# The first attention of a two-layer decoder, reordered into pairs and quads of heads

## What is computed

```python
scores = jnp.einsum('bhtd,bhsd->bhts', q, k) * ATTNSCALE          # q and k after rope
key_self = jnp.clip(jnp.sum(k * k, axis=-1), 1e-06, None)
w = jax.nn.softplus(scores / jnp.sqrt(key_self)[:, :, None, :])
w = jnp.where(causal, w, 0.0)
w = w * jax.nn.sigmoid(SCALE * w)
w = jnp.where(w < sinks, 0.0, w)
total = jnp.sum(w, axis=-1, keepdims=True) + sinks + 1e-06
out = jnp.einsum('bhts,bhsd->bhtd', w / total, v) + (sinks / total) * v_null
y = mean over the branches of (context @ W_O + W_O_bias)
```

## Time and profile before

| | us |
|---|---|
| time before, median of 3 runs (lowest to highest) | 3647.07 (3644.27 to 3649.19) |
| the profiled execution, its own time | 3643.7 |
| its span from the first to the last instruction | 3642.0 |
| first start of L434 and of L651 | 64.0, 67.0 |
| last start of L651 | 1119.5 |
| layer norm behind the first attention starts | 1188 |

### The profile page before, as it was taken

How to read it: one execution, slowest core, us unless ns; L and a number is a source line. 1 busy time by engine, 2 the same in 40 slices (tenths; PEclk the granted TensorE clock), 3 DMA queues, 4 the chain that set the end, 5 groups by cost and what they waited for, 6 DMA issues and landing times. The chain is left out here.

```text
span 3642.0 us, 51017 instructions
## 1 busy us (share of the span) xinstructions
PE 3184.4 (87%) x16640; PEld 2118.5 (58%) x16640; DVE 2152.4 (59%) x4638; ACT 1572.6 (43%) x2705; POOL 895.5 (25%) x1150
## 2 busy tenths in 40 slices
PE   5899999999987455898997999999999899986998
PEld 3334334334432343666665268888888677755887
DVE  3998898898885444655654134444444544445544
ACT  3665665665662212444443133333333455543211
POOL 2333334333331000444443000000000355550000
PEclk9999999999997666999998589999999899997999
DMA  2000000000000102010012000000000200001000
GB/s 87 3 4 1 3 3 0 3 3 0 3 1 1 38 23 61 20 37 23 21 37 56 0 4 3 3 3 3 3 3 5 75 6 6 3 29 59 6 6 26
DMA packets 88113, 61.03 MB, mean 17 GB/s; under 512 B 54800, under 2 KB 76560, under 8 KB 87504
## 3 DMA queue, kind: packets, MB, share of 16 engines
q1 hardware_dynamic: 88016, 59.93, 5.5%
HBM read 41.03 MB, written 8.39 MB: 14 GB/s over the span
## 5 line engine op out<-in xcount | busy, mean ns | idle before, releaser
L1727 POOL TENSOR_SCALAR x_weights<-x_weights,x_sums 128x256 f32<-128x256 f32 x256 | 231.7, 923 | 1061.6 <-DVE x_sums L1764 1061.6
L632 DVE SCALAR_TENSOR_TENSOR a_w<-a_w,a_sinks 128x256 f32<-128x256 f32 (+1 forms) x1024 | 466.3, 515 | 3.2
L434 ACT ACTIVATE a_e<-psum 128x1536 f32<-128x1536 f32 x128 | 185.6, 1450 | 385.6 <-PE psum L401 385.3
L318 PE MATMUL psum<-a_w,a_v 128*17 128x512 f32 x512 | 273.7, 617 | 85.4 <-DVE a_sumT L623 67.9
L1029 POOL TENSOR_SCALAR f_weights<-f_weights,f_sums 128x256 f32<-128x256 f32 x256 | 232.1, 924 | 294.8 <-DVE f_sums L1259 294.8
L476 POOL TENSOR_SCALAR_AFFINE_SELECT a_w<-a_w 128x512 f32<-128x512 f32 x256 | 180.1, 725 | 383.9 <-DVE a_w L651 383.8
L1456 ACT ACTIVATE a_weights<-psum,a_negmax 128x1024 f32<-128x1024 f32 x128 | 142.6, 1114 | 293.1 <-DVE a_negmax L1496 293.1
L399 PE MATMUL psum<-a_qT,a_kT_head 128*128 128x512 f32 x512 | 251.7, 614 | 7.7 <-DVE a_w L651 5.0
L1430 PE MATMUL psum<-a_v,a_turned_w 128*128 128x128 f32 x2048 | 248.3, 275 | 0.0
L651 DVE SCALAR_TENSOR_TENSOR a_w<-a_e,psum 128x1536 f32<-128x1536 f32 x128 | 223.9, 1749 | 24.9 <-ACT a_e L436 22.2
L1430 PEld LDWEIGHTS psum<-a_v,a_turned_w 128*128 128x128 f32 x2048 | 238.1, 192 | 0.0
(11 more groups left out here) (300 smaller groups left out, 6913.6 us busy)
## 6 DMA issues: line engine op xcount, KB each, us to landing
a_xnT<-all_xnT_all SPq DMA_DIRECT2D x16, 256.0 KB, 2.3
x_ctxT<-in_x_ctxT SPq DMA_DIRECT2D x16, 256.0 KB, 2.7
f_xnT<-all_xnT_all SPq DMA_DIRECT2D x16, 256.0 KB, 2.3
f_pv_rows<-f_pv SPq DMA_DIRECT2D x8, 512.0 KB, 2.8
f_pv_groups<-f_pv_rows SPq DMA_DIRECT2D x8, 512.0 KB
f_w<-in_f_w SPq DMA_DIRECT2D x2, 2048.0 KB, 10.4
all_x_all<-in_x SPq DMA_DIRECT2D x1, 2048.0 KB, 8.5
a_wq<-in_a_wq SPq DMA_DIRECT2D x2, 1024.0 KB, 10.4
```

Source lines behind the costliest of these rows:

```text
L318: pe.matmul(psO[0:DH + 1, :], v1[:, 0, u, :], w[:, u % RING, half * 512:(half + 1) * 512], start=True, stop=False)
L434: act.activation(e[:, j % 2, :], psS[j % 2], ACT.Exp).then_inc(exp_done, 1)
L632: ins = dve.scalar_tensor_tensor(part, part, sinks[:, r * NH + u:r * NH + u + 1], part, ALU.is_ge, ALU.mult)
L1727: ins = pool.tensor_scalar(w, w, sums[:, k, h, t:t + 1], None, ALU.mult)
```

## The change

Heads are worked in pairs (eight steps a batch, three slots a step) and summed in quads.

- **Scores.** The pair of step s is head 4*(s//2) + s%2 and that head plus two. Each lies in 32 rows of its own; `kT_half` holds k twice, with the even and with the odd heads' rows zero, so that a product uses 32 rows instead of 128. A slot is two PSUM banks, 1024 columns: slots 0 and 1 hold two branches each of both heads (first 128 keys, 256 queries), slot 2 all four branches of both (last 128 keys, last 128 queries). There are three such slots in place of two groups of three banks.
- **Causal part.** A further product, of the identity and a matrix with -1e30 above the diagonal, both float32r, is added onto the scores of each bank. The selections of GpSimd go.
- **ScalarE** takes exponential and logarithm by slot, 1024 columns, 24 times a batch; silus come in bursts of four heads at the first slot of every even step, once the last merge of the step before is there.
- **VectorE** merges by slot (two instructions of 512 columns in slots 0 and 1, one of 1024 in slot 2), runs the 16 thresholds of a quad (one of 384 columns for each head and branch) in one piece at the first slot of an even step, and copies sums of 128 x 512 after the first and second slot of odd steps.
- **Sums.** For four heads, each half is four products of 32 columns on 32 partitions of their own in bank 6, then four more for the last keys.
- The order written out by hand becomes `BESIDE_SLOT`. In it TensorE scores slot x of step s+1 after the side items of (s, x), and needs the merge of (s, x) for it; in odd steps a half of the sums follows that score.
- GpSimd masks k four times a batch, not sixteen.

```diff
-NU = NH
-RING = 8
-K1 = BR * T
-UNIT = BR * T + BR * P
+PAIRS_OF_HEADS, QUADS, SLOTS = NH // 2, NH // 4, 3
+PAIR_RING = 4
...
-SOFTPLUS_LAG, THRESHOLD_LAG, SUM_LAG = 1, 6, 8
-SILU_EVERY, SILU_FROM, SILU_TO = 4, 5, 2
...
+BESIDE_SLOT = {(0, 0): [("q", 0, HERE)], (0, 1): [("q", 1, HERE)], (0, 2): [("q", 2, HERE)],
+               (1, 0): [("q", 3, HERE)], (1, 1): [("regroup", 4, OLD), ("regroup", 5, OLD)], (1, 2): [("k", 0, AHEAD)],
+               (2, 0): [("k", 1, AHEAD)], (2, 1): [("v", 0, HERE)],
+               (3, 0): [("regroup", 6, OLD), ("regroup", 7, OLD)], (3, 1): [("norm", 0, AHEAD)], (3, 2): [("q", 0, AHEAD)],
+               (4, 0): [("q", 1, AHEAD)], (4, 1): [("q", 2, AHEAD)], (4, 2): [("q", 3, AHEAD)],
+               (5, 0): [("turn", 0, OLD)], (5, 1): [("turn", 1, OLD)], (5, 2): [("turn", 2, OLD)],
+               (6, 0): [("turn", 3, OLD)], (6, 1): [("out", 0, OLD)], (6, 2): [("regroup", 0, HERE), ("regroup", 1, HERE)],
+               (7, 0): [("regroup", 2, HERE), ("regroup", 3, HERE)]}
...
+def quad_at(b, at, new, old):
+    if at >= 0:
+        return (at, b * QUADS + at) if new else None
+    return (QUADS + at, b * QUADS + at) if old else None
...
-        psS = [psum[:, 3 * i:3 * i + 3, :].rearrange("p k n -> p (k n)") for i in range(2)]
+        psS = [psum[:, 2 * x:2 * x + 2, :].rearrange("p k n -> p (k n)") for x in range(SLOTS)]
...
+            def score_slot(bb, step, x):
+                n, g = bb * PAIRS_OF_HEADS + step, step // 4
+                if x == 0 and step % 4 == 0:
+                    pe.wait_ge(kheads_ready, bb * 2 + g + 1)
+                    pe.wait_ge(rotated, bb * ROTATED + 6 + 4 * g)
+                if not isinstance(n, int) or n > 0:
+                    pe.wait_ge(capped, (n - 1) * SLOTS + x + 1)
+                heads = [4 * (step // 2) + step % 2 + 2 * h for h in range(2)]
+                rows = [slice(32 * (u % 8 // 2), 32 * (u % 8 // 2) + 32) for u in heads]
+                if x < 2:
+                    for h in range(2):
+                        pe.matmul(psum[:, 2 * x + h, :], kT_half[rows[h], step % 2, g, 0:P], qT[rows[h], g, 2 * x:2 * x + 2, :],
+                                  start=True, stop=False)
+                    for h in range(2):
+                        ins = pe.matmul(psum[:, 2 * x + h, :].rearrange("p (r t) -> p r t", r=2)[:, :, 0:P], ident_r[:],
+                                        future[:].unsqueeze(1).to_broadcast([P, 2, P]), start=False, stop=True)
+                else:
+                    for h in range(2):
+                        pe.matmul(psum[:, 4 + h, :], kT_half[rows[h], step % 2, g, P:T], qT[rows[h], g, :, P:T],
+                                  start=True, stop=False)
+                    for h in range(2):
+                        ins = pe.matmul(psum[:, 4 + h, :].rearrange("p (r t) -> p r t", r=BR), ident_r[:],
+                                        future[:].unsqueeze(1).to_broadcast([P, BR, P]), start=False, stop=True)
+                ins.then_inc(scored, 1)
...
+            def sum_half(b, quad, half):
+                k, n = quad
+                if k == 0 and half == 0:
                     pe.wait_ge(v_taken, b + 1)
                 pe.wait_ge(weights_done, n + 1)
                 wait(pe, sums_taken, 2 * n + half)
-                pe.matmul(psO[0:DH + 1, :], v1[:, 0, u, :], w[:, u % RING, half * 512:(half + 1) * 512],
-                          start=True, stop=False)
-                lo = K1 + half * 256
-                pe.matmul(psO[0:DH + 1, :].rearrange("p (r t) -> p r t", r=2)[:, :, P:T], v1[:, 1, u, :],
-                          w[:, u % RING, lo:lo + 256].rearrange("p (r t) -> p r t", r=2), start=False, stop=True)\
-                  .then_inc(summed, 1)
+                for tile in range(TT):
+                    for h4 in range(4):
+                        branches = w[:, (2 * k + h4 % 2) % PAIR_RING, h4 // 2, 2 * half:2 * half + 2, :]
+                        out = psO[VCOLS * h4:VCOLS * h4 + VCOLS, :].rearrange("p (r t) -> p r t", r=2)
+                        cols, to = (slice(0, T), out) if tile == 0 else (slice(T, COLS), out[:, :, P:T])
+                        ins = pe.matmul(to, v1[:, tile, 4 * k + h4, :], branches[:, :, cols], start=(tile == 0),
+                                        stop=(tile == TT - 1))
+                ins.then_inc(summed, 1)
...
+                        spare_free = [(out_taken, bb + 1)]
+                for step in range(PAIRS_OF_HEADS):
+                    quad = quad_at(b, (step - 3) // 2, new, old) if step % 2 else None
+                    for x in range(SLOTS):
+                        for kind, i, when in BESIDE_SLOT.get((step, x), []):
+                            if exists[when]:
+                                pass_through_spare(kind, i, when)
+                        if step < PAIRS_OF_HEADS - 1 and new:
+                            score_slot(b, step + 1, x)
+                        elif step == PAIRS_OF_HEADS - 1 and ahead:
+                            score_slot(b + 1, 0, x)
+                        if quad and x < 2:
+                            sum_half(b, quad, x)
...
+                for step in range(PAIRS_OF_HEADS):
+                    for x in range(SLOTS):
+                        n = (b * PAIRS_OF_HEADS + step) * SLOTS + x
+                        if new:
+                            act.wait_ge(scored, n + 1)
+                            act.activation(e[:, x, :], psS[x], ACT.Exp).then_inc(exp_done, 1)
+                            act.wait_ge(exp_done, n + 1)
+                            act.activation(e[:, x, :], e[:, x, :], ACT.Ln, bias=1.0).then_inc(ln_done, 1)
+                        for kind, i, when in BESIDE_SLOT.get((step, x), []):
+                            if exists[when]:
+                                take_turned(kind, i, when)
+                        if ahead and (step, x) == (3, 2):
+                            act.wait_ge(norm_taken, b + 2)
+                            act.activation(ksq[:], ksq[:], ACT.Ln).then_inc(ln_k, 1)
+                            act.wait_ge(ln_k, b + 2)
+                            act.activation(ksq[:], ksq[:], ACT.Exp, scale=-0.5, bias=ln_quarter[:, 0:1]).then_inc(knorm_ready, 1)
+                        quad = quad_at(b, step // 2 - 1, new, old) if (step % 2, x) == (0, 0) else None
+                        if quad:
+                            k, n = quad
+                            act.wait_ge(capped, (n * 2 + 2) * SLOTS)
+                            for pair in range(2):
+                                for h in range(2):
+                                    wu = w[:, (2 * k + pair) % PAIR_RING, h].rearrange("p r t -> p (r t)")
+                                    act.activation(wu, wu, ACT.Silu, scale=SILU_SCALE).then_inc(silu_done, 1)
                             act.preload_act_table_set("natural_log_exp_and_others")
...
-            def head_rows(g, first, last):
-                for u in range(8 * g + first, 8 * g + last):
-                    ins = pool.tensor_scalar(kT_head[:, u, :], kT[:, g, :], head_mask[:, u % 8:u % 8 + 1], 1.0,
+            def head_rows(g):
+                for odd in range(2):
+                    ins = pool.tensor_scalar(kT_half[:, odd, g, :], kT[:, g, :], parity[:, odd:odd + 1], 1.0,
                                              ALU.mult, ALU.mult)
-                    if u % 8 == 7:
-                        ins.then_inc(kheads_ready, 1)
+                ins.then_inc(kheads_ready, 1)
...
+            def take_sums(quad, half):
+                k, n = quad
+                dve.wait_ge(summed, 2 * n + half + 1)
+                if half == 0:
+                    wait(dve, regrouped, (n - 1) * 2)
+                dve.tensor_copy(sumT[:, k % 2, half * 512:(half + 1) * 512], psO).then_inc(sums_taken, 1)
+            def threshold(quad):
+                k, n = quad
+                for pair in range(2):
+                    for h in range(2):
+                        dve.wait_ge(silu_done, n * 4 + 2 * pair + h + 1)
+                        for r in range(BR):
+                            part = w[:, (2 * k + pair) % PAIR_RING, h, r, :]
+                            col = r * NH + 4 * k + pair + 2 * h
+                            ins = dve.scalar_tensor_tensor(part, part, sinks[:, col:col + 1], part, ALU.is_ge, ALU.mult)
+                ins.then_inc(weights_done, 1)
...
+                for step in range(PAIRS_OF_HEADS):
+                    summed_quad = quad_at(b, (step - 3) // 2, new, old) if step % 2 else None
+                    silu_quad = quad_at(b, step // 2 - 1, new, old) if step % 2 == 0 else None
+                    for x in range(SLOTS):
+                        n = (b * PAIRS_OF_HEADS + step) * SLOTS + x
+                        if new:
+                            if x == 0 and step % 2 == 0:
+                                wait(dve, summed, (b * QUADS + step // 2 - 1) * 2)
+                            dve.wait_ge(ln_done, n + 1)
```

(38 more changed lines are left out.)

167 lines of the change are left out of this document (32 added, 135 removed).

## The result

| | before | after |
|---|---|---|
| time, median (lowest to highest) | 3645.8 us (3644.3 to 3649.2) | 3693.3 us (3682.0 to 3699.2) |
| ratio, 95% interval | | 1.0127 (1.0103 to 1.0151) |
| span of the profiled execution | 3642.0 | 3697.3 |
| main part, first exponential to end of the last merge | 1057.2 | 1130.7 |
| tail behind it, to the end of the last addition onto x | 66.7 | 39.2 |

What follows compares the result with a forecast made beforehand. TensorE and VectorE fill the first attention before; afterwards no engine is full and the strict order decides. Eight batches of 132.4 us less 21 give 1038 against 1057, the tail 43 against 66.7: 43 off, 3604 us, range 3500 to 3690.

Steps and rivals of the forecast that it cites:

- the clock's charge: TensorE work behind the hole in three of four quads runs at the lower clock: 2 us each, 6 a batch.
- Its bound, 139 a batch: Upper end for a batch: 13 us of TensorE's chain work at the lower clock throughout, less the 2 charged.
- Rival C: First attention: the clock stays down through the odd step, 5 us more a quad, +20 a batch, 3764 us; chance 0.11.
- The walk's total: First attention: following the strict order through a batch's four quads at the priced engine times gives 126.4 us a batch.
- VectorE's sum 86: VectorE's work in a batch of the first attention falls from 124 to 86 us.
- ScalarE's 86: ScalarE's batch work: exponentials and logarithms 49 us, silus with table loads 33, with small ones some 86.
- the hole of 7.4 us: TensorE idles 7.4 us waiting for the merge behind the 16 thresholds, in three of four quads.
- the score slot 1.5: TensorE takes 1.5 us for each of the first two score slots, 1.7 for the third.
- the copies' idle time of 3.1 us twice a quad: VectorE idles 3.1 us at each copy of sums while TensorE scores, then sums; twice a quad.
- TensorE's 87 us: TensorE's batch work in the first attention: scores 38 us, sums 12, other matmuls 37, together 87.
- Rival B: Column tiles of the sums don't run four abreast: +10 a batch, 3684 us, or +30, 3840; chance 0.11.
- Rival A: Orders interlock better, so the longest engine sets a batch: 86 becomes some 97 us, time 3321; chance 0.10.

Runs made afterwards that it cites:

- e6_warm: Changed kernel plus idle TensorE products in every larger gap: 8 or 4 a hole, one in each odd-step gap and between two regroupings; 3590.2 us.
- e8_rows128: Changed kernel with score products taking all 128 rows in place of 32, running one after another; 3701.7 us.
- e9_again32: Changed kernel with each pair of 32-row score products issued twice, the second overwriting the first; 3912.7 us.
- e1_fill7: Changed kernel with seven idle fp32 products in TensorE's hole before the score of slot 1 in steps 0, 2 and 4; 3687.6 us.
- e10_oddonly: Changed kernel with idle products only in the odd steps' gaps and between two regroupings of step 1, holes left empty; 3708.4 us.

## Why the prediction was wrong

**The step that failed** is the clock's charge: "I charge 2 us for each such quad ... That is 6 a batch". By the account it is 21.9 a batch, half of 43.8; by batches alone, 144.5 less the 124.5 at clock 1.00 in e6_warm, 20.0. Two things were wrong in the step. It took only the work right behind a hole, "about 4 us", while the clock stayed low 5.5 to 14.8 us into the work. And it took holes alone, while the clock also falls behind gaps of 1.4 to 2 us in the odd steps. Its bound, 139 a batch, was passed as well.

Rival C came nearest, with +20 a batch on top of the 6, but not quite as it was put: its sign was that the passes stay at twice their length until the next burst, and in most quads the clock comes back and falls again; only the stretch at 677.26 is of C's kind. The argument against it ("keeps TensorE almost without a gap for 14 us, and today's stage, with gaps of its own, stands at 0.99") did not look at how long the falls last. Today's stage has them too, 3.4 us each; in the steady batch of the changed kernel they last 6.8 us and more. Today's scores use 128 rows, the new ones 32, and e8_rows128 against e9_again32 shows that this matters. C's price was somewhat too high and its chance, 0.11, too low.

**What held.** The walk's total: 126.4 a batch forecast, 124.5 in the batch of e6_warm at clock 1.00 with the change's own order, 122.6 by the chain's account of the changed kernel. That it came so near is partly luck. From one silu burst to the next that batch takes 32.4, 30.5, 33.8 and 27.8 us in steps 0 and 1, 2 and 3, 4 and 5, 6 and 7, where the walk had 32.8, 30.3, 30.4 and 32.9: 3.4 too little in one quad and 5.1 too much in another. (The changed kernel itself, with its clock, has 40.1, 37.1, 37.2 and 28.9.) VectorE's sum 86 (85.7), in which the thresholds are 36 us and not 34, the merges 30 and not 29 (the prediction's own prices add up to 30), and the takes that stay, by difference, 14 and not 18. ScalarE's 86 (84.9), the hole of 7.4 us (7.9), the score slot 1.5 (1.48), the copies' idle time of 3.1 us twice a quad (3.2). TensorE's 87 us at full speed cannot be read from a busy time of 106.3 at 0.77.

Rival B falls: half a quad's sums cost 1.43 us, where one head's took 1.40, so four column tiles run side by side without loss. By the Trainium skill (TensorE: Matmul & The Clock Gate, Part 3), which has 2.38 times for three tiles, I had estimated 0.35 us more a half; the measurement decides against that here. Rival A falls too: no batch of this order came under 122 even without cold time.

**The sum again**, in spans. Predicted 3599 (3642.0 less 43), measured 3697.3, so 98.3 off. Clock 8 x (21.9 - 6) = +127; walk 8 x (122.6 - 126.4) = -30; the ends, where 8 x 144.5 less 1130.7 is 25 and not 21, -4; tail 39.2 for 43, -4; start 62.4 for 64.0, -2; everything behind the first attention 2465.0 for 2454.1, +11. That is +98. The last term I count as spread: with the same code behind the first attention these traces have from 2454 to 2472 us there, the one of the kernel before the least.

**Where the gain of the real work went.** At the clock of before, the batch would be 122.6 against 134.7, 97 us in eight, and the tail's 27 with it. 8 x 21.9, less the 8 x 1.7 that before pays itself, took 162 back, and the ends of the main part 9 more (8 batches less the main part are 34 us before, 25 after): the first attention is 46 us longer. The span grew by 55, with the 11 of the unchanged stages and an attention that starts 1.6 earlier; the medians differ by 47.

## What to carry to other kernels

When a change empties TensorE, price its clock as a term of the path: all TensorE work on the chain up to the next rise, not only the few microseconds behind the hole, and count short gaps too. To test it, fill every gap with idle products into a free bank: if the time falls and the rest of the engines' work stays the same, the clock was the cause; filling only some of the gaps can show nothing, as e1_fill7 and e10_oddonly did. And compare batches of one trace that differ in clock alone. A hand-over in which the waiting engine's product is issued behind another's is worth turning round first; here that was 91 us for moving two lines.

## What the runs showed that I had not expected

- Work that nobody reads made a kernel faster by 103 us (3693.3 to 3590.2) and, with the other order, by 84 (3601.8 to 3518.0).
- The granted clock fell behind gaps of 1.4 to 2 us. It does so in the kernel before too, behind six of its eleven gaps of 2.1 to 2.3 us, but for 3.4 us each (0.99 in the mean); in the steady batch of the changed kernel, with 32-row scores and 32-column sums, it stays low for 6.8 us and more.
- The same gap was followed by a fall in one batch and not in another: 1.4 us in e6_warm and in e1_fill7.
- The same lengthening of a slot gave clock 0.88 as 128-row and 0.76 as 32-row products, 3701.7 against 3912.7 us.
- Three holes of 8 us a batch made into four of 4, with more gaps of 1.2 to 2.3 us, lowered the clock from 0.77 to 0.73.
